# The expert products of a sorted mixture of experts as three single-pass products of high and low parts

## The reference

```
x = x + mixer_and_mlp(layernorm(x))
h = layernorm(x)                                   # (2048, 512)
probs = softmax(h @ Wr)                            # 8 experts; the best 2 of each row, weights made to sum to 1
y_e = (silu(h @ Wg[e]) * (h @ Wu[e])) @ Wd[e]      # Wg, Wu: 512 x 352; Wd: 352 x 512
out = x + sum over the row's two experts of weight * y_e
```

## Time and profile before

| | us |
|---|---|
| median of 3 runs | 1512.77 (1512.68 to 1512.79) |
| the profiled execution | 1511.89 |
| its span, first to last instruction | 1510.2 |
| TensorE busy / DVE / ACT / POOL | 1439.8 / 781.1 / 446.8 / 431.5 |
| mean granted clock | 0.984 |

### The profile page before, as it was taken

One profiled execution on the slowest core, in us unless ns is written; L12 is line 12 of the kernel. 1 busy time (PEld: TensorE's weight loads), 2 busy tenths in 40 slices (PEclk: granted clock), 3 DMA queues, 4 the chain that ended last, 5 costly groups with the idle time before them and its releaser, 6 DMA issues.

```text
span 1510.2 us, 19850 instructions
## 1 busy us (share of the span) xinstructions
PE 1439.8 (95%) x6903; PEld 1058.4 (70%) x6903; DVE 781.1 (52%) x1258; ACT 446.8 (30%) x927; POOL 431.5 (29%) x457
## 2 busy tenths in 40 slices
PE   6899999799999997999999999999988999999995
PEld 4677878566666666888888888888867665665663
DVE  6979678689999993333332333333468222222221
ACT  4444445545555553211111121111121111111110
POOL 2502111257777662101011011101011232332331
PEclk9999999899999999999999999999999999999998
DMA  9123124622332215010000000210376233333322
GB/s 197 61 107 112 57 84 142 200 91 105 122 117 99 99 64 203 28 28 29 14 28 28 14 28 22 71 40 0 133 245 233 45 57 65 70 57 66 63 38 34
DMA packets 84354, 124.41 MB, mean 82 GB/s; under 512 B 27695, under 2 KB 44079, under 8 KB 84272
## 3 DMA queue, kind: packets, MB, share of 16 engines
q1 hardware_dynamic: 71488, 103.62, 21.0%
q0 software_dynamic: 8736, 18.62, 7.2%
q10 hardware_dynamic: 4048, 1.10, 0.3%
HBM read 81.37 MB, written 43.78 MB: 83 GB/s over the span
## 4 chain that ended last, share of the span: by engine, by line
PE 59%; DVE 1%; DMA 1%; issue 0%; ACT 0%; POOL 0%; POOLq 0%; ACTq 0%; DVEq 0%
PE fin_bank L1811 35%; PE fin_bank L1952 12%; PE fin_bank L1972 6%; PE fin_bank L1942 1%; PE fin_bank L1921 1%; PE fin_bank L1961 1%; PE fin_bank L1934 0%; DMA out_dram<-result_rows,put_idx 0%; PE fin_bank L1879 0%; DMA xs<-xn_rows,idx 0%; PE fin_bank L1867 0%; PE fin_bank L1986 0%; DVE ff_w_lo L1607 0%; DVE fi_bn L1642 0%; ACT ff_w_hi L1531 0%
## 5 line engine op out<-in xcount | busy, mean ns | idle before, releaser
L1811 PE MATMUL fin_bank<-ff_hT_hi,ff_w_hi 128*128 128x512 f32 x512 | 202.7, 396 | 3.2 <-DVE ff_w_lo L1577 3.2
L1811 PE MATMUL fin_bank<-ff_hT_lo,ff_w_hi 128*128 128x512 f32 x512 | 202.4, 395 | 0.0
L1811 PE MATMUL fin_bank<-ff_hT_hi,ff_w_lo 128*128 128x512 f32 x512 | 202.4, 395 | 0.0
L1952 PE MATMUL fin_bank<-wx,xT 128*128 x624 | 194.3, 465 | 0.8 <-ACT xT L1546 0.8
L1569 DVE TENSOR_TENSOR ff_prod<-ff_prod,fin_bank 128x512 f32<-128x512 f32 x64 | 44.0, 688 | 262.7 <-PE fin_bank L1811 262.7
L1418 POOL TENSOR_TENSOR ff_w_lo<-ff_stage,ff_w_hi 128x1024 fp32r<-128x1024 f32 (+1 forms) x24 | 56.5, 2358 | 410.3 <-ACT ff_w_hi L1521 405.9
L1952 PEld LDWEIGHTS fin_bank<-wx,xT 128*128 128x128 f32 x624 | 117.3, 193 | 60.2 <-issue 3.7
L646 PE MATMUL pj_bank<-hT_hi,w_in_hi 128*128 128x512 f32 x336 | 136.3, 406 | 6.8 <-POOL w_in_lo L294 4.1
L541 DVE SCALAR_TENSOR_TENSOR conv_acc<-raw,conv_w,conv_acc 128x512 f32<-128x512 f32 x144 | 115.7, 804 | 41.7 <-ACT raw L347 35.6
L646 PE MATMUL pj_bank<-hT_lo,w_in_hi 128*128 128x512 f32 x336 | 133.4, 397 | 0.0
L646 PE MATMUL pj_bank<-hT_hi,w_in_lo 128*128 128x512 f32 x336 | 132.7, 395 | 0.0
(11 more groups left out here) (287 smaller groups left out, 2501.9 us busy)
## 6 DMA issues: line engine op xcount, KB each, us to landing
cv_rows<-cst SPq DMA_DIRECT2D x12, 1024.0 KB, 4.3
cv<-cv_rows SPq DMA_DIRECT2D x16, 768.0 KB, 4.3
zs_rows<-zst SPq DMA_DIRECT2D x8, 1024.0 KB, 6.5
zs<-zs_rows SPq DMA_DIRECT2D x16, 512.0 KB, 5.2
wx<-in_L_ffn_Wg_dram SPq DMA_DIRECT2D x8, 704.0 KB, 8.5
wx<-in_L_ffn_Wu_dram SPq DMA_DIRECT2D x8, 704.0 KB, 9.0
w_raw<-in_L_attn_in_proj_w_dram SPq DMA_DIRECT2D x32, 128.0 KB, 3.7
x<-_attn_hidden_states_dram SPq DMA_DIRECT2D x16, 256.0 KB, 5.4
```

Of the source, the lines that this page charges most:

```text
L1811: mm = eng.matmul(ps, w[a], x[b], start=first and i == 0, stop=last and i == 2)
L1952: mm = eng.matmul(ps[:, 0:EI], xT[j % 2][:, k, :], wx[:, bass.ds(e, 1), at:at + EI].rearrange("p a n -> p (a n)"), start=(k == 0), stop=(k ...
```

## The change

The expert products are made with `three` as well, from high and low parts:

- A new constant `KS = 3`: of the four blocks of 128 rows of Wg and Wu, three are split; the fourth stays a plain fp32 product (2 instructions) with `xe_raw`. Wd is split whole.
- For every tile ACT copies the weights of its expert into high parts (`weights_high`: gate 1056, up 1056, down 1536 numbers per partition) and DVE subtracts to get low parts (`weights_low`). There is one buffer for each kind: a high part is overwritten only when TensorE has done with the one of the tile before (`ge(eng, s[done], j)`). The rows and the inner activations are split in the same way (`turned`, `width_high`, `width_low`; 384 numbers).
- `weighted` moves from DVE to ACT. `wide` is cut into a gate and an up half, and `turn_x(j + 2)` stands between them; both halves wait for their low weights (`ew_lo`).
- On DVE `weights_low` of gate and up of tile 0 stand ahead of the 17 small steps that lead to list 2, and `turned(0)` behind them.
- Every engine that needs the expert's number reads it into a register once for each tile (`owner`), some tiles ahead: DVE and ACT three, TensorE two.
- The gathers run five tiles ahead instead of three; the fourth and fifth are issued only after list 2, since their memory and that of `wd_hi` is where the one-hot matrices lay.
- ACT fills rows 96 to 127 of the last block of Wd with zeros, once (4,096 numbers per partition), right after the exponential of the routing.
- At the end of `project`, TensorE makes 14 fp32 products of 128 columns that nobody reads.

```diff
@@ project, end of TensorE's block
+            for i in range(14):
+                eng.matmul(turn[1][:, 0:P], ones[:, :], ident[:, :], start=True, stop=True)
@@ finish
+        order = [("gate", 0), ("up", 0), ("gate", 1), ("up", 1)]
+        for j in range(SORT_TILES):
+            order += [("down", j)] + [(w, j + 2) for w in ("gate", "up") if j + 2 < SORT_TILES]
+        nth = {piece: i + 1 for i, piece in enumerate(order)}
+        def owner(eng, j):
+            return eng.value_load(tile_expert[0:1, j:j + 1], min_val=0, max_val=E - 1)
@@ GpSimd
+            eng.wait_ge(s["table"], 2)
+            eng.memset(xs3[:, :], 0.0).then_inc(s["const"], 1)
+            eng.wait_ge(s["const"], 15)
             eng.wait_ge(s["ids"], 3)
+            gather(3)
+            gather(4)
             for j in range(SORT_TILES):
-                if j + 3 < SORT_TILES:
-                    gather(j + 3)
+                if j + 5 < SORT_TILES:
+                    gather(j + 5)
@@ ScalarE
+            eng.activation(wx[EI % P:P, :, DN + (NC - 1) * D:DN + NC * D],
+                           ones[EI % P:P, 0:1].unsqueeze(2).broadcast_to([P - EI % P, E, D]), ACT.Copy, scale=0.0)\
+               .then_inc(s["exp_spare"], 1)
+            def weights_high(kind, j):
+                done = {"gate": "eg_ps", "up": "eu_ps", "down": "y_ps"}[kind]
+                ge(eng, s[done], j)
+                eng.activation(high[kind], raw_part(own[j], kind), ACT.Copy).then_inc(s["ew_hi"], 1)
...
             for j in range(SORT_TILES):
+                weights_high("down", j)
+                if j + 3 < SORT_TILES:
+                    own[j + 3] = owner(eng, j + 3)
+                width_high(j)
                 if j + 1 < SORT_TILES:
                     gate(j + 1)
                 if j + 2 < SORT_TILES:
                     turned(j + 2)
+                    weights_high("gate", j + 2)
+                if j:
+                    weighted(j - 1)
+                if j + 2 < SORT_TILES:
+                    weights_high("up", j + 2)
+            weighted(SORT_TILES - 1)
@@ VectorE
+            def weights_low(kind, j):
+                eng.wait_ge(s["ew_hi"], nth[kind, j])
+                eng.tensor_tensor(low[kind], raw_part(own[j], kind), high[kind].bitcast(F32), ALU.subtract)\
+                   .then_inc(s["ew_lo"], 1)
...
+            weights_low("gate", 0)
+            weights_low("up", 0)
...
+            turned(0)
...
+            turned(1)
+            weights_low("gate", 1)
             product(0)
             put_list()
+            weights_low("up", 1)
             for j in range(SORT_TILES):
-                turned(j)
+                weights_low("down", j)
+                if j + 3 < SORT_TILES:
+                    own[j + 3] = owner(eng, j + 3)
+                width_low(j)
+                if j + 2 < SORT_TILES:
+                    turned(j + 2)
                 if j + 1 < SORT_TILES:
                     product(j + 1)
-                weighted(j)
+                if j + 2 < SORT_TILES:
+                    weights_low("gate", j + 2)
+                    weights_low("up", j + 2)
@@ TensorE
+            def wide(j, kind):
...
+                eng.wait_ge(s["ew_lo"], nth[kind, j])
+                for k in range(KS):
+                    mm = three(ps[:, 0:EI], x, w, k == 0, k == KD - 1)
+                for k in range(KS, KD):
+                        mm = eng.matmul(ps[:, 0:EI], xe_raw[j % 2][:, (k - KS) * P:(k - KS + 1) * P],
+                                        wx[:, bass.ds(own[j], 1), at:at + EI].rearrange("p a n -> p (a n)"),
+                                        start=False, stop=(k == KD - 1))
             for j in range(SORT_TILES):
                 turn_width(j)
+                if j + 2 < SORT_TILES:
+                    own[j + 2] = owner(eng, j + 2)
                 if j + 1 < SORT_TILES:
-                    wide(j + 1)
+                    wide(j + 1, "gate")
                 if j + 2 < SORT_TILES:
                     turn_x(j + 2)
+                if j + 1 < SORT_TILES:
+                    wide(j + 1, "up")
                 down(j)
```

More of the change, by code:

```diff
@@ L1550, in gate, with width_high, weighted @@
                 ge(eng, s["hT_ps"], j - 1)
-                eng.activation(act_g[j % 2][:, :], eg_ps[j % 2][:, 0:EI], ACT.Silu).then_inc(s["esilu"], 1)
+                eng.activation(act_g[j % 2][:, 0:EI], eg_ps[j % 2][:, 0:EI], ACT.Silu).then_inc(s["esilu"], 1)
+            def width_high(j):
+                eng.wait_ge(s["hT_ps"], j + 1)
+                ge(eng, s["y_ps"], j - 1)
+                eng.activation(h_hi[j % 2][:, :, :].rearrange("p c n -> p (c n)"), hT_ps[:, 0:NC * P], ACT.Copy)\
+                   .then_inc(s["eh_hi"], 1)
+            def weighted(j):
+                eng.wait_ge(s["y_ps"], j + 1)
+                ge(eng, s["put"], 16 * (j - 1))
+                eng.activation(rows[j % 2][:, :], y_ps[j % 2][:, :], ACT.Copy, scale=wt[:, j:j + 1]).then_inc(s["sum"], 1)
+            eng.wait_ge(s["route"], R_TE)
+            eng.wait_ge(s["wx_dma"], 16 * 4 * E)
+            for i in range(2):
+                eng.wait_ge(xn_dma[i], 16 * (NR // 2))
+            own = {j: owner(eng, j) for j in range(3)}
+            weights_high("gate", 0)
+            weights_high("up", 0)
             turned(0)
@@ L1943, in turn_x @@
                 last.then_inc(s["xT_ps"], 1)
[L1945 to L1950 removed]
+            def wide(j, kind):
+                i, ps, free, done = {"gate": (0, eg_ps[j % 2], "esilu", "eg_ps"), "up": (1, eu_ps[j % 2], "eh", "eu_ps")}[kind]
+                if i == 0:
+                    eng.wait_ge(s["ex_lo"], j + 1)
+                eng.wait_ge(s["ew_lo"], nth[kind, j])
+                ge(eng, s[free], j - 1)
+                for k in range(KS):
+                    w = [t[:, i, k * EI:(k + 1) * EI] for t in (gu_hi, gu_lo)]
+                    x = [t[j % 2][:, k, :] for t in (xe_hi, xe_lo)]
+                    mm = three(ps[:, 0:EI], x, w, k == 0, k == KD - 1)
+                if KS < KD:
+                    for k in range(KS, KD):
@@ L1957, in turn_width @@
+                mm.then_inc(s[done], 1)
             def turn_width(j):
                 eng.wait_ge(s["eh"], j + 1)
-                ge(eng, s["hT"], j)
-                for c, (i, n) in enumerate(IC):
-                    last = eng.transpose(hT_ps[0:n, c * P:(c + 1) * P], act_g[j % 2][:, i:i + n], ident[:, :])
+                ge(eng, s["eh_lo"], j)
+                for c in range(NC):
+                    last = eng.transpose(hT_ps[:, c * P:(c + 1) * P], act_g[j % 2][:, c * P:(c + 1) * P], ident[:, :])
@@ L1980, in _ @@
             eng.wait_ge(s["route"], R_TE)
-            wide(0)
+            own = {j: owner(eng, j) for j in range(2)}
+            wide(0, "gate")
             turn_x(1)
+            wide(0, "up")
             eng.wait_ge(s["onehot"], 9)
```

121 lines of the change are left out of this document (73 added, 48 removed).

## The result

| | before | after |
|---|---|---|
| median of 4 runs each, us | 1512.72 | 1470.38 (1468.75 to 1470.92) |
| the profiled execution | 1511.89 | 1470.92 |
| its span | 1510.2 | 1469.2 |

The ratio is 0.972, with a 95% interval from 0.9708 to 0.9732: 42.3 us faster. 1473 was forecast.

The account below looks back on a forecast made before the run. The prediction took TensorE alone to bound the expert loop: 38 periods shorter by 1.09 us (-41.4), beginning +0.7, end +1.8, project -1.0, together -39.9, hence 1473 us. Its 8-in-10 range was 1462 to 1492.

Parts of the forecast that it names:

- Pace: TensorE's expert loop: an fp32r product takes 0.164 us at 352 columns and 0.231 at 512; period 6.99 against 8.09.
- DVE and ACT: Expert loop: straight lines from earlier rows give DVE 5.92 and ACT 5.94 us a period, both under TensorE's 6.99.
- the 0.4 to spare at the low gate: Expert loop's tightest place: DVE ends the low gate at 6.9 us, TensorE wants it at 7.32.
- B: Rival, expert loop: DVE fills the period; low weight parts longer by half need 8.1 us, total 1514; chance in full 0.03.
- Its small form: Low weight parts a tenth to a fifth longer, or 0.5 us of register load uncovered: period 7.2 to 7.5, 1481 to 1492; 0.12.
- Register loads: Expert loop, DVE and ACT: loads behind the longest pieces are covered up to about a microsecond; taken as nothing.
- C: Rival, POOL's puts: 0.6 us longer makes its loop 6.1; with a third such delay 7.3, total 1484; chance 0.05.
- D: Rival, expert loop: DVE's low parts and POOL's transfers exclude each other, DVE needs 8.49 us, total 1529; chance 0.03.
- End: Behind the expert loop: put of tile 37 at 3.6 us, the last 5.50 later at 9.1 instead of 7.24; +1.8.
- Beginning and project: Expert loop's start: later `turned(0)`, +0.7 (0 to +2); end of `project`: 14 products may keep the clock up, -1.0 (0 to 3).
- Gathers: POOL in the expert loop: the gathers, five ahead, have periods to land; no cost in the sum.
- Sum: Whole kernel: -41.4 + 0.7 + 1.8 - 1.0 = -39.9 us, giving 1473.

Follow-up runs that it names:

- widths: Changed kernel with the 14 products at the end of `project` replaced by 56 fp32r products of 512 down to 128 columns: 1475.19 us in one run.
- dve_big: Changed kernel with four added DVE operations of 128 numbers between the product and the low gate in each period: 1489.91 us, ratio 0.9853.
- no_warm: Changed kernel without the 14 products at the end of `project`: 1472.35 us, ratio 0.9737.
- early_last: Changed kernel with ACT's weighted rows right behind the high inner width and the last tile's down parts in gate and up's buffers: 1468.63 us, ratio 0.9709.
- one_input: Changed kernel with DVE's low weight parts made from one input, the raw weights times zero, instead of a subtraction: 1470.12 us, ratio 0.9721.
- ks2: Changed kernel with two of the four blocks of Wg and Wu split instead of three (`KS = 2`): 1476.97 us, ratio 0.9769.
- depth3: Changed kernel with the gathers three tiles ahead instead of five: 1583.03 us, ratio 1.0473.

## Why the prediction was right

**The forecast held, and by its own steps.** TensorE bounds the loop before and after, the gain is the count of its products, and DVE fills to just under the period.

- *Pace.* 0.164 was taken, on the view that 0.017 of the 512-column pace is per instruction. widths shows that it scales: 0.159. This term was mis-sized: the period came out at 6.95 instead of 6.99. That is some 1.4 us of the 1.6 by which the loop beat its forecast. The figure of the Trainium skill (TensorE: Matmul & The Clock Gate, Back-to-back issue gap), which is for a single product by itself and names no data type, gives an estimate of 0.216 at 512 columns and 0.149 at 352. Both are under the measured values, 0.232 and 0.159; by it the gain would have been overstated by some 14 us (57 against 43).
- *DVE and ACT.* The straight lines of the earlier trace rows gave 1.26 and 1.76; 1.252 and 1.759 were measured. ACT's weighted rows were 0.09 over. The order laid out by hand held to about a tenth: of the 0.4 to spare at the low gate dve_big finds 0.29. B was the live rival. No low part was longer than its line, so it didn't come, and dve_big shows what a longer DVE chain costs. Its small form was priced too high by the prediction's own layout: a fifth on the low gate is 0.25 us, which that margin takes up, and not a period of 7.2 to 7.5.
- *Register loads.* Taken as nothing because of the cover, which is right: no gap shows behind the low down. With less cover a load leaves DVE 0.25 to 0.29.
- *C and D.* Puts do get longer, by the 0.6 foreseen (2.22 against 1.59), and have 3 us of cover. I had put D aside because in rows 7 the two ran side by side and neither waited for the whole of the other. For POOL that was the wrong reading: the gather of 1170.53 found L1764 with 0.76 to run and took 0.61 more than the one before it, which is the wait for DVE's end, less 0.12, to within 0.03. The rule behind D, the Trainium skill's (SBUF — State Buffer, SBUF: two separate sides), says that such instructions take turns by whole instructions. POOL's waits agree with it, DVE's don't. What D had wrong is that side's price: POOL's instruction lasts 1.04 or 1.59, but holds DVE back for 0.07 at most, so DVE needs 5.9 a period and not 8.49.
- *End.* +1.8 forecast, +2.8 measured. I took the put of tile 37 as free to start behind its rows, 3.6 behind the turn. Its rows ended on time (at 2.7, with 2.8 laid out), but it waited for the landing of the put of 36, and that for the put of 35, which DVE's low part had made 0.65 longer. The rows of 36 and 37 come only 5.4 to 5.6 behind those of the tile before, since ACT has no x and no high gate of a further tile ahead of them. The term was built from one put, and the chain reached three back.
- *Beginning and project.* +0.7 and -1.0 taken, +0.2 and -1.2 measured, within the bounds given. TensorE's 28 halves end at 283.26, 0.82 before it is needed, and the clock gain is no_warm's window. That -1.2 lies so near to -1.0 is luck: by where list 1 starts in the variants with the same code ahead of it, anything from -1.8 to +0.3 could have been read.
- *Gathers.* "The gathers, five ahead, have periods to land" is right, but I let it pass as a convenience, and that is luck. It carries 113 us: had the change left three ahead, my sum would have said 1473 and the chip 1583. I laid one period of ACT, DVE and TensorE out, but not POOL's queue, where each gather stands behind a put. The loop ACT, put, gather, turned x, ACT closes over a number of tiles that the depth sets.
- *Sum.* The terms are off by 1.1 together: the loop by -1.6, the end by +1.0, the beginning by -0.5, project by -0.2, and +0.2 behind the last put. The median lies 2.6 under 1473 because the profiled execution lay 0.9 under its median before and 0.5 above it now.

What stays open: whether early_last is faster than the changed kernel as a time, what the 14 products are worth, and what decides the clock in the first expert period.

## What to carry to other kernels

When work moves to another engine's queue, follow every ring that runs through it: sum one lap, divide by the number of tiles that the buffering lets it span, and compare that with the period. Depth that looks idle in the kernel before can be what the new order stands on. Where several transfers must follow each other's landing, cost the end of the loop by that pace from the last place where it had slack, not from the last transfer alone.

## What the runs showed of the hardware

- A back-to-back fp32r product took 0.45 to 0.46 ns a column from 512 down to 256, with a floor near 0.11 us below that (0.109 at 192), where the weight loads lie too (0.113 in the earlier trace rows).
- An indirect transfer issued by POOL waited for the end of the running DVE subtraction of two SBUF operands (less 0.12 us: 0.64 for 0.76 left, 1.58 for 1.70), and beside one_input's operation with one SBUF operand too (0.09 for 0.21); DVE lost 0.07 at most. Beside the product, which reads PSUM, it didn't wait (ks2's put, 1.55 with 0.42 left).
- TensorE's clock was lower after short idle times too. In depth3, with 0.5 to 3.9 us idle before each `turn_x`, it was 1.00 from 1302.33 to 1313.27, with 2.28 idle in it, and 0.70 from there to 1323.50, with 3.31 idle. The changed kernel's last down products, after 3.71 us idle, have a mean granted clock of 0.58 (1451.72 to 1455.20), and most of them, at the lower level, followed each other at 0.43 instead of 0.23.
